# Relaying five of eight normaliser chunks through memory in a linear-attention and mixture-of-experts kernel

## The reference

```python
qkv = x @ W_qkv                                   # 16 heads of 64
q, k = relu(q @ W_f + b_f), relu(k @ W_f + b_f)   # per head
kv = einsum('bhnd,bhne->bhde', k, v)
out = einsum('bhnd,bhde->bhne', q, kv)
normalizer = einsum('bhnd,bhd->bhn', q, k.sum(axis=2))
out = out / (normalizer[..., None] + 1e-6)
x = layernorm(x + out @ W_out + b_out)
probs = softmax(x @ gate_w.T)                     # 8 experts, the best 2 are taken
y = sum over the 2 of prob * (gelu(x @ w1[e] + b1[e]) @ w2[e] + b2[e])
x = layernorm(x + y)
```

## Time and profile before

| what | us |
|---|---|
| median of 3 runs (range) | 456.76 (455.43 to 457.03) |
| the profiled execution | 455.49 |
| its span, first to last instruction | 453.7 |
| PE busy | 426.3 |
| DVE busy | 323.0 |
| ACT busy | 276.7 |
| POOL busy | 162.5 |

### The profile page before, as it was taken

How to read it: one execution, slowest core, us unless ns; L and a number is a source line. 1 busy time by engine, 2 the same in 40 slices (tenths; PEclk the granted TensorE clock), 3 DMA queues, 4 the chain that set the end, 5 groups by cost and what they waited for, 6 DMA issues and landing times.

```text
span 453.7 us, 8859 instructions
## 1 busy us (share of the span) xinstructions
PE 426.3 (94%) x2784; PEld 340.6 (75%) x2784; DVE 323.0 (71%) x937; ACT 276.7 (61%) x554; POOL 162.5 (36%) x164
## 2 busy tenths in 40 slices
PE   7899999999999999999999999889999999999940
PEld 6777677677676676676776656479999999999940
DVE  3846968968968968968968998665774434456785
ACT  4755666666667666656756655349555655555565
POOL 3111002332331331431431421055777755555550
PEclk9999999999999999999999999999999999999985
DMA  8990210200200200200100060499696999498534
GB/s 215 315 217 3 75 65 0 95 24 2 94 25 0 95 24 1 94 26 1 72 24 1 25 241 16 143 344 304 173 242 219 284 380 311 134 362 311 180 114 139
DMA packets 40013, 61.16 MB, mean 135 GB/s; under 512 B 6287, under 2 KB 27284, under 8 KB 39840
## 3 DMA queue, kind: packets, MB, share of 16 engines
q1 hardware_dynamic: 30992, 50.00, 35.2%
q0 software_dynamic: 4544, 8.54, 5.4%
q10 hardware_dynamic: 4432, 2.07, 1.5%
HBM read 44.55 MB, written 17.49 MB: 137 GB/s over the span
## 4 chain that ended last, share of the span: by engine, by line
PE 85%; DVE 7%; DMA 3%; ACT 2%; issue 1%; ACTq 1%; POOL 0%; POOLq 0%; DVEq 0%; SPq 0%
PE psO L583 11%; PE psA L473 10%; PE psA L474 10%; PE psA L475 10%; PE psG L715 9%; PE psS L715 6%; PE psA L562 5%; PE psG L473 4%; PE psG L605 3%; PE psG L474 3%; PE psG L475 3%; PE psG L574 3%; PE psA L630 3%; DMA cst<-consts 2%; PE psS L519 1%
## 5 line engine op out<-in xcount | busy, mean ns | idle before, releaser
L433 POOL DMA_INDIRECT expert_rows<-rows,pos x64 | 62.0, 969 | 101.0 <-PE psA L475 65.1
L458 POOL DMA_INDIRECT expert_results<-q_act,kT x56 | 55.3, 988 | 36.7 <-DVE q_act L1237 26.4
L738 ACT ACTIVATE kT<-psA,bf_col 128x512 f32<-128x512 f32 x64 | 44.0, 688 | 34.8 <-PE psA L475 34.4
L583 PE MATMUL psO<-qn,mixed 128*128 128x512 f32 x128 | 64.2, 594 | 0.0
L738 ACT ACTIVATE q_act<-psA,bf_col 128x512 f32<-128x512 f32 x64 | 44.1, 689 | 26.1 <-PE psA L475 25.6
L904 DVE TENSOR_TENSOR k_lo<-psA,k_hi 128x512 fp32r<-128x512 f32 x64 | 43.9, 687 | 8.2 <-ACT k_hi L738 7.8
L715 PE MATMUL psG<-x_raw,q_act 128*128 x384 | 46.9, 275 | 0.2 <-ACT q_act L878 0.2
L1131 DVE TENSOR_TENSOR qn<-q_act,psG 128x512 f32<-128x512 f32 x64 | 42.9, 681 | 5.1 <-PE psG L574 5.0
L715 PEld LDWEIGHTS psG<-x_raw,q_act 128*128 128x128 f32 x384 | 44.9, 192 | 0.6 <-issue 0.6
L562 PEld LDWEIGHTS psA<-cst,kT 128*128 128x128 f32 x256 | 31.3, 140 | 16.0 <-issue 4.6
L738 ACT ACTIVATE k_hi<-psA 128x512 fp32r<-128x512 f32 x64 | 38.3, 598 | 7.3 <-PE psA L562 7.2
(11 more groups left out here) (202 smaller groups left out, 1045.5 us busy)
## 6 DMA issues: line engine op xcount, KB each, us to landing
k_hi<-expert_weights SPq DMA_DIRECT2D x15, 578.0 KB
k_lo<-expert_weights SPq DMA_DIRECT2D x15, 578.0 KB, 5.3
w_more<-expert_weights SPq DMA_DIRECT2D x9, 578.0 KB, 5.2
expert_weights<-w_more SPq DMA_DIRECT2D x8, 512.0 KB, 2.9
kT<-expert_rows SPq DMA_DIRECT2D x28, 132.0 KB, 4.7
w_raw<-w SPq DMA_DIRECT2D x8, 256.0 KB, 3.4
x_raw<-w SPq DMA_DIRECT2D x1, 2048.0 KB, 9.8
x<-expert_results SPq DMA_DIRECT2D x4, 512.0 KB, 5.8
```

The lines of the kernel that those rows point to most:

```text
L433: pool.indirect_dma_start(xs, bass.IndirectOffsetOnAxis(ap=pos_2[o % 2][:, j, k:k + 1], axis=0), rows_2[o % 2][:, j, k, :], None).then_inc ...
L458: pool.indirect_dma_start(ys, bass.IndirectOffsetOnAxis(ap=xrow[r][:, c, D:D + 1].bitcast(I32), axis=0), yrow[u][:, c, :], None, bounds_ch ...
L583: mm(psO[:, :], mixed[:, c, :], qn[:, c % 4, :], start=c == 0, stop=c == CH - 1).then_inc(o_pe, 1)
L738: return act.activation(out_, in_, func, **kw)
```

## The change

1. **Relay.** For batches 0 to 6 the normalisers of chunks 3 to 7 no longer go through `spread_norm`. SP writes the chunk's two rows of `rn` eight times over into memory (`normalisers`) and reads them back copied to 64 partitions each. Batch 7 keeps eight spreads. The copies lie in a new tile `bc` (chunks 3 and 4), in the tokens `x_raw` of the finished batch (chunk 5), and in the gram `gm` (chunks 6 and 7).
2. **Queue order.** The copies of the split expert weights stand between the relays on SP, and the 2 MB load waits until batch 6's queries are normalised.
3. **One product.** `turn_gate` is the identity with the gate weights beside it (136 columns), so that four fp32 products give turned tokens and logits. Scaling the logits takes two DVE operations instead of one; `first_norm` on ACT waits for them, and `ranks` for `first_norm`.
4. **ACT.** The two halves of `r_hi` and `r_rest` move around the second gram copy: in batch 7 both before it, in the others one before it.
5. **Experts.** `turn_rows(0)` and its `xT_lo` move into call 8, ahead of the last two outputs. On DVE the logits of batch 7 come one block later. The last two blocks are taken in halves.
6. The late table's scratch moves to `gm` and `mixed`.

```diff
+RELAYED = 3
+COPIES = 8
+HALVED = NBLK - 2
...
+        rs = nc.dram_tensor("normalisers", [CH - RELAYED, 2, COPIES, S], F32, kind="Internal").ap()
...
-        gwc = sb("gwc", [P, E])
+        turn_gate = sb("turn_gate", [P, P + E])
...
+        bc = sb("bc", [P, 2, S])
...
+        z_at = [psO[:, j * (D + E):(j + 1) * (D + E)] for j in range(TILES - 1)] + [psS[:, (2 * TILES + 1) * E:(2 * TILES + 1) * E + D + E]]
...
+        def copies_at(c, p):
+
+            return (bc[:, 0, :], bc[:, 1, :], x_raw[:, p * TILES:(p + 1) * TILES, :].rearrange("p t d -> p (t d)"),
+                    gm[:, 0:S], gm[:, S:])[c - RELAYED]
...
-            return psX2[bank_of(n)][:, 0:D] if n == NBLK - 1 and t else psY2[bank_of(n)][:, t, :]
+            return psX2[bank_of(n)][:, 0:D] if n >= HALVED and t else psY2[bank_of(n)][:, t, :]
...
-            for ex in range(E):
+
+            def keep_split(ex):
                 sp.wait_ge(w1_l, ex + 1)
                 sp.dma_start(wb[ex, :, 0:2 * F], w1_split[ex % 2].bitcast(F32)).then_inc(w1_out[ex % 2], 16)
                 if ex + 2 < E:
                     load_w1(ex + 2)
+
+            for b in range(B):
+                for ex, _ in SPLIT_AT.get(b, ()):
+                    keep_split(ex)
+                if b < B - 1:
+                    sp.wait_ge(n_step, N_STEPS * (b + 1))
+                    for c in range(RELAYED, CH):
+                        row = c % 4 * QUAD + 2 * c
+                        sp.dma_start(rs[c - RELAYED], rn[row:row + 2, 1, None, :].broadcast_to([2, COPIES, S])).then_inc(r_out[c - RELAYED], 16)
+                    for c in range(RELAYED, CH):
+                        if c == CH - 2:
+                            sp.wait_ge(m_pe, 2 * (b + 1))
+                        sp.wait_ge(r_out[c - RELAYED], 16 * (b + 1))
+                        sp.dma_start(copies_at(c, b), rs[c - RELAYED][:, :, None, :].broadcast_to([2, COPIES, DH // COPIES, S])).then_inc(bc_in[c - RELAYED], 16)
+            sp.wait_ge(qn_done, CH * (B - 1))
...
                 for j in range(TILES):
-                    last = mm(psS_l[:, j, :], zT[:, j * P:(j + 1) * P], gwc[:, :], start=True, stop=True)
-                last.then_inc(l_pe, 1)
-                for j in range(TILES):
-                    last = pe.transpose(psO_z[:, j, :], zT[:, j * P:(j + 1) * P], con("ident"))
+                    last = mm(z_at[j], zT[:, j * P:(j + 1) * P], turn_gate[:, :], start=True, stop=True)
                 last.then_inc(z_pe, 1)
...
-                    if prev and c + 1 < CH:
+                    if prev and c + 1 < (RELAYED if cur else CH):
                         spread_norm(c + 1)
...
+                    if b == B and c == CH - 1:
+                        turn_rows(0)
...
+                    gram_copy(0)
+                    if prev:
+                        fill(p)
+                    act.wait_ge(r_l, b)
+                    norm_half(0)
+                    if b == B - 1:
+                        norm_half(1)
+                    gram_copy(1)
+                    if b < B - 1:
+                        norm_half(1)
...
-                    dve.tensor_tensor(qn[:, c % 4, :], q_act[:, c, :], psG[:, c % 2, :], ALU.mult).then_inc(qn_done, 1)
+                    dve.tensor_tensor(qn[:, c % 4, :], q_act[:, c, :], copies_at(c, p) if relayed else psG[:, c % 2, :], ALU.mult).then_inc(qn_done, 1)
...
-                if 2 <= n <= NBLK:
+                if 1 <= n < NBLK:
+                    rows_low(n)
+                if n == 2:
+                    scale_logits(B - 1)
+                if 2 <= n < HALVED + 2:
                     result(n - 2)
-                if n == NBLK + 1:
+                if n >= HALVED + 2:
                     for c in range(2):
-                        last_result(c)
+                        last_result(n - 2, c)
                 if n == 1:
                     means(B - 1)
-                    scale_logits(B - 1)
```

More of the change, by code:

```diff
@@ L198, in program @@
         endi = sb("endi", [1, E], I32)
-        past = [sb(f"past{i}", [1, LATE * len(ERAS) * E]) for i in range(2)]
+        past = [sb(f"past{i}", [1, EARLY * 2 * E]) for i in range(2)]
         tab = sb("tab", [1, 3, NBLK])
@@ L258, in program @@
             sem(n) for n in ("ksum_done", "ks_done", "n_pe", "n_step", "qn_done", "o_pe", "zT_done"))
[L260 to L261 removed]
+        z_pe, c_pe, st_step, ln_step, x1_done, route, exp_done, table = (
+            sem(n) for n in ("z_pe", "c_pe", "st_step", "ln_step", "x1_done", "route", "exp_done", "table"))
         e_x, e_w, e_out = ([sem(f"{n}{u}") for u in range(ROW_SLOTS)] for n in ("e_x", "e_w", "e_out"))
@@ L270, in program @@
         in_xr0, in_fold_q, in_fold_v, tab_step = (sem(n) for n in ("in_xr0", "in_fold_q", "in_fold_v", "tab_step"))
+        r_out, bc_in = ([sem(f"{n}{c}") for c in range(CH - RELAYED)] for n in ("r_out", "bc_in"))
         r_h, r_l, bc_pe, in_spread, spread_ready = (sem(n) for n in ("r_h", "r_l", "bc_pe", "in_spread", "spread_ready"))
@@ L672, in attention @@
                     mix(1)
-            for b in range(B + 1):
-                attention(b)
             def turn_rows(n):
@@ L715, in second_layer @@
                         last = mm(result_at(n, t), hT[v][:, c, t * P:(t + 1) * P], w2_all[:, ds(expert * (FC * D) + c * D, D)], start=c == 0, stop=c == FC - 1)
-                    if n == NBLK - 1 and t == 0:
+                    if n >= HALVED and t == 0:
                         last.then_inc(e_half, 1)
                 last.then_inc(e_down, 1)
+            for b in range(B + 1):
+                attention(b)
             for n in range(NBLK + 2):
-                if n < NBLK:
+                if 1 <= n < NBLK:
                     turn_rows(n)
@@ L837, in attention, with gram_copy @@
                         exponents(p)
-                    for h in range(2):
+                    def gram_copy(h):
                         act.wait_ge(g_pe, 2 * b + h + 1)
@@ L842, in attention, with norm_half @@
                         hi(gm[:, h * 512:(h + 1) * 512], psG[:, h, :]).then_inc(g_done, 1)
-                        if h == 0 and prev:
-                            fill(p)
-                    act.wait_ge(r_l, b)
-                    for h in range(2):
+                    def norm_half(h):
                         half = slice(h * S // 2, (h + 1) * S // 2)
@@ L978, in summed @@
             def summed(to, by, n, k):
-                table_, scaled = (past[i][:, 0:n * k].rearrange("p (n k) -> p n k", k=k) for i in range(2))
+                table_, scaled = ((past if n == EARLY else late_past)[i][:, 0:n * k].rearrange("p (n k) -> p n k", k=k) for i in range(2))
                 tb(dve.tensor_tensor(scaled, table_, by[:, None, 0:k].broadcast_to([1, n, k]), ALU.mult))
@@ L1050, in __init__ @@
                 def __init__(self, o):
-                    self.o, self.step = o, Steps(dve, route, ROUTE_STEPS * o + 1)
+                    self.o, self.step = o, Steps(dve, route, ROUTE_STEPS * o + 2)
                 def pick(self):
@@ L1126, in normalise @@
                 def normalise(c):
-                    dve.wait_ge(bc_pe, CH * p + c + 1)
+                    relayed = cur and c >= RELAYED
+                    if relayed:
+                        dve.wait_ge(bc_in[c - RELAYED], 16 * (p + 1))
+                    else:
+                        dve.wait_ge(bc_pe, RELAYED * p + c + 1)
                     if c >= 4:
                         dve.wait_ge(o_pe, CH * p + c - 3)
-                    dve.tensor_tensor(qn[:, c % 4, :], q_act[:, c, :], psG[:, c % 2, :], ALU.mult).then_inc(qn_done, 1)
+                    dve.tensor_tensor(qn[:, c % 4, :], q_act[:, c, :], copies_at(c, p) if relayed else psG[:, c % 2, :], ALU.mult).then_inc(qn_done, 1)
                 def key_lo(c):
```

49 lines of the change are left out of this document (28 added, 21 removed).

## The result

The changed kernel takes **448.94 us** (median of 4 runs, 448.42 to 449.82) where the kernel before takes 456.31 (455.43 to 457.03, 4 runs): a ratio of 0.9841, interval 0.9814 to 0.9868. It is faster by 7.4 us (1.6%) and not by the 13 us forecast, and lies outside the range of 440.8 to 447.5. The profiled execution took 449.82 us, its span is 448.0 us against 453.7: 5.7 us less.

The account below looks back on a forecast made before the run. The prediction took PE to bound mid-attention, with DVE already bounding call 7. Its terms, 6.9 + 2.0 + 0.98 + 1.05 + 0.9 + 0.9 = 12.7 us, led from 455.49 to 442.8 us; it took 443.3, range 440.8 to 447.5.

Parts of the forecast that it names:

- Do the copies arrive?: Relay in attention: chunk 3's copies land 2.0 us before DVE's product needs them, so waiting costs nothing.
- formula for late copies: If DVE is late by L, calls 1 to 6 change by L - 1.48 us each and call 7 by L.
- the first rival: Copies come late and DVE waits at chunk 3: 462.5 us, chance 0.05; mild form, L around 1.5, 451 us, chance 0.03.
- relay, calls 1 to 6: Attention: five spreads of 0.23 us leave PE in each call, saving 6.9 us if DVE keeps up.
- joint product, calls 1 to 7: One product for turned tokens and logits saves 0.25 us each time, 1.75 us over these calls.
- call 8, up to its first spread: PE's wait for `r_hl` ahead of the first spread goes, saving 0.98 us.
- entry up to block 4, with batch 7's joint product: Start of the experts: waits for `xT_lo` of blocks 0 and 2 shrink; 2.2 us including the product.
- last two blocks: End of the kernel: taking blocks in halves lets DVE and POOL start earlier, saving 0.9 us.
- What PE saves by a spread: Attention: each spread taken off PE saves 0.23 us.
- Does DVE keep up?: Attention: of DVE's 1.48 us slack the relay takes 1.15, leaving 0.33; relayed products cost the same.
- The second rival: DVE becomes the bound if each of the five products costs 0.2 us more: 448.3 us, chance 0.10.
- the expert blocks take up a wait that isn't there now: Expert blocks: one of the signs named as showing the prediction wrong; no size given.

Follow-up runs that it names:

- e14: The changed kernel without its relay, all eight chunks going through the spread: 449.41 us, ratio 0.9845 to the kernel before.
- e15: The changed kernel with each relay write storing four copies instead of eight: 443.30 us, ratio 0.9723 to the kernel before.
- e4: The changed kernel with four chunks (4 to 7) relayed instead of five: 444.37 us, ratio 0.9735 to the kernel before.
- e6: The changed kernel with only the last block in halves, as before the change: 448.44 us, ratio 0.9821 to the kernel before.
- e7: The changed kernel with POOL scattering batch 7's rows two per block in blocks 4 to 7, not one per block in 4 to 11: 447.51 us.
- e12: The changed kernel with four copies instead of eight and batch 7's scatters two to a block: 442.18 us, ratio 0.9691 to the kernel before.
- e2: The changed kernel with chunk 3's read behind three writes instead of five: 474.46 us on a core where the kernel before took 484.83, ratio 0.9768.
- e10: The changed kernel with four copies per write instead of eight, on a core where the kernel before took 484.83 us: 472.10 us, ratio 0.9752.

## Why the prediction was wrong

The failed step is **"Do the copies arrive?"**. "The first read is issued ... at about 108.54 + 2.2, and lands at 114.2", 5.7 us after the reciprocals. In call 3, the latest, it landed 9.3 us after them. Three sizes were off:

- SP's time for a write: 0.4 us taken from the earlier trace rows, whose transfers start from memory and go to 128 partitions; 0.84 us measured (4.19 for five). The read was issued 2.1 us later than forecast.
- The read: 3.4 us from the earlier trace rows, measured 5.0. By the account above two of the 5.0 us are the five writes ahead of it on two engines.
- The reciprocals end 0.95 us after the first product of `mix` (107.42 against 106.47); before it was 0.49.

2.1 + 1.6 + 0.5 against 2.0 us of reserve makes DVE 2.1 us late in call 3: its product stands 10.26 us behind the start of `mix` instead of 8.13. The prediction's formula for late copies then gives 2.13 - 1.48 = 0.65 us of loss there, less 0.35 for the joint product: 0.30; measured 0.19. In the other calls up to 6 the product is 0.4 to 1.6 us late, and the formula comes within 0.15 us of each. So the mechanism of the first rival, in its mild form, is what happened. It had a chance of 0.03. It gave 451 us, with L at 1.5 in all seven calls; L was 0.4 in call 1 and nothing in call 7.

The prediction had the cause in hand. It estimated three microseconds for the five writes on two engines, and let "the first chunk land half a microsecond later", as if they held up the first read's issue alone. The 436 GB/s behind that estimate, from the Trainium skill (DMA: Bandwidth & Descriptors, "Anatomy of one DMA — SWDGE (gpsimd) path"), would leave 54 GB/s for two engines. The writes ran at 27 to 29, and the measurement decides: they take 6 us, and a read spread over sixteen engines needs the two that they hold.

The sum, step by step, on the profiled executions:

| step | forecast | measured |
|---|---|---|
| relay, calls 1 to 6 | 6.9 | 1.1 (e14's 205.24 less 204.18); 6.8 in e15 |
| relay, call 7 | 0 | 0 (0.31 in all, 0.33 in e14 without a relay) |
| joint product, calls 1 to 7 | 1.75 | 2.4 (207.36 - 205.24 + 0.31) |
| call 8, up to its first spread | 0.98 | 1.05 (2.95 to 1.90 from the start of `mix`) |
| entry up to block 4, with batch 7's joint product | 2.2 | 2.5 (22.26 to 19.74) |
| blocks 4 to 38 | 0 | -1.2 (6.40 us early to 5.21); -0.4 to -0.7 in e4, e6, e14 and e15, +0.4 in e7 and e12 |
| last two blocks | 0.9 | 0.5 (5.21 to 5.67) |
| start-up, up to the first `mix` | 0 | -0.7; the sixteen kernels reach it at 38.8 to 40.4 us, so this is scatter |
| sum | 12.7 | 5.7 |

- **What PE saves by a spread** was right: 1.13 us for five.
- **Does DVE keep up?** Right: with the copies in time calls 1 to 6 take 33.08 us, and relayed products last as long as others. Groups of DVE by form (ns least/median/most):

```profile
L1178 DVE TENSOR_TENSOR qn<-q_act,psG x29: 666/680/689, 43.4 to 289.4; 128x512 f32<-128x512 f32 x29
L1178 DVE TENSOR_TENSOR qn<-q_act,bc x14: 680/690/693, 48.1 to 256.8; 128x512 f32<-128x512 f32 x14
L1178 DVE TENSOR_TENSOR qn<-q_act,gm x14: 670/682/692, 54.6 to 263.9; 128x512 f32<-128x512 f32 x14
```

  The second rival falls. The Trainium skill's rule against two SBUF operands (GPSIMD Engine Reference, section 1, Specifications) was not put to the test, however: no tensor operation of POOL overlaps a relayed product in the changed kernel (in batch 3 the nearest ends at 111.93), and beside them POOL issues scatters.
- **The joint product** was too small by 0.1 us a time: the first three of the four take 0.70 us (129.60 to 130.30), 0.23 each, as forecast, but the next query product starts only 0.14 us behind the fourth.
- **Call 8 and the entry** were right within 0.4 us.
- **Blocks 4 to 38** were missing from the sum. The prediction named "the expert blocks take up a wait that isn't there now" as what would make it wrong, and such a wait came, at block 17. It could have read from the trace before that POOL falls behind there (3.9 us a block beside PE's 3.4) and that the turn of block 17 starts 2.93 us behind the issue of its load. The wait does not follow the lead: e4 and e15, 4.9 and 6.0 us ahead of the changed kernel there, wait 0.88 and 0.28 us.
- **The last two blocks**: the stores came 1.1 us closer, but only 0.5 us of it reached the end, and e6 gives the halves of block 37 0.2 to 0.3. DVE's last normalisation is 6.57 us earlier, ACT's, behind its three outputs, 5.53. That ACT keeps the rest is read from the trace; no run takes these outputs away.

Added up: 5.8 us of relay lost, 1.6 us in the expert blocks behind the entry and 0.7 in the start-up, against 1.1 us more from the joint product, call 8 and the entry. With the first put right (e15) the kernel takes 443.3 us. That this is the forecast number is in part luck, since the other errors run against each other.

## What to carry to other kernels

A relay through memory has three prices: the issue on its queue, the trip, and the transfers that are still under way on the engines it needs. Cost the write by the number of partitions that it starts from (here two partitions used two engines), and look at the DMA share while it runs. Weigh the number of copies both ways: each one lengthens the write, and with too few the read goes to fewer engines. Four were better than eight here, one was far worse. A read that an engine waits for goes ahead of writes that are needed later (e2). And before a change moves an engine ahead, look for loads that it meets with little reserve: such a wait differed here from kernel to kernel by up to 1.2 us, whatever the lead.

## What the runs showed of the hardware

- Writes of two partitions ran at 27 to 29 GB/s on two engines, reads of two rows at 49 GB/s on two engines: such a write goes at little more than half the rate of such a read. Why is open.
- A write's time on SP's queue grows with what is queued: 0.29 us with one copy (4 KB), 0.66 with four, 0.84 with eight, 1.55 with sixteen (7.74 us for five); within five writes of 64 KB it goes from 0.66 to 2.38 us.
- Fewer rows in memory than engines is not always slower (e10): with four copies a read is spread over 8 rows, the DMA share from 112 to 115 us is 0.57 instead of 0.94, and the copies arrive sooner, because less is written ahead of them.
